# A graph layer and a mixture of experts on one core: late node blocks on two pairs of PSUM banks, 128-row routing scatters, and sort scatters released by TensorE's step signals

## What is computed

```python
def gnn(h, (ei, ej), d2):
    x = concat(h[ei], h[ej], d2)
    msg = silu(x @ mW1 + mb1)
    msg = layer_norm(msg, ln_g, ln_b)
    msg = silu(msg @ mW2 + mb2)
    agg = segment_sum(msg, ei, 6250)
    return h + silu(concat(h, agg) @ uW1 + ub1) @ uW2 + ub2

def moe(tokens):                       # 8 experts, the best 2 of each token
    probs = softmax(tokens @ router_w.T)
    rw, re = top_k(probs, 2);  rw = rw / sum(rw)
    combine = zeros(N, 8) with rw at re
    for e in range(8):
        y = gelu(tokens @ w1[e] + b1[e]) @ w2[e] + b2[e]
        out = out + combine[:, e] * y  # out starts as tokens
    return out

x = x + gnn(_layernorm(x), (src, dst), edge_weight1)
x = x + moe(_layernorm(x))
```

## Time and profile before

| | |
|---|---|
| device time, three runs | 2866.51, 2866.66, 2869.15 us; median 2866.66 |
| profiled execution | 2863.55 us; its span in the profile 2861.8 us |
| busy share of the span | PE 84%, DVE 71%, ACT 53%, POOL 46% |
| mean granted TensorE clock | 0.914 of full speed |
| sort's last matmuls end | 547.2 us |
| late node blocks | 547 to 614 us |
| record conversion | 614.35 to 626.4 us |
| messages, update, router | 626.5 to 2390 us |
| routing scatters | 2392.3 to 2544.4 us |
| first expert matmul, end of span | 2550.2, 2861.8 us |

### The profile page before, as it was taken

One profiled execution on the slowest core, in us unless ns is written; L12 is line 12 of the kernel. 1 busy time (PEld: TensorE's weight loads), 2 busy tenths in 40 slices (PEclk: granted clock), 3 DMA queues, 4 the chain that ended last, 5 costly groups with the idle time before them and its releaser, 6 DMA issues. The chain is left out here.

```text
span 2861.8 us, 60909 instructions
## 1 busy us (share of the span) xinstructions
PE 2391.6 (84%) x15142; PEld 2054.4 (72%) x15143; DVE 2041.0 (71%) x6013; ACT 1506.1 (53%) x5127; POOL 1314.9 (46%) x1333
## 2 busy tenths in 40 slices
PE   4388888768999999999999999999999990039990
PEld 4277777637888888888888888888887880028880
DVE  8989989647777777777777777777777665323335
ACT  2522122237777777777777777777775650013330
POOL 2055555615555555555555555555552114754440
PEclk7599999879999999999999999999999995569995
DMA  6010001123233332223333233323342771333338
GB/s 140 3 30 24 27 24 30 40 81 93 88 90 90 90 90 87 88 89 90 90 89 90 86 88 90 90 88 90 91 84 44 229 239 46 85 93 124 118 104 270
DMA packets 159889, 259.19 MB, mean 91 GB/s; under 512 B 39875, under 2 KB 105088, under 8 KB 159447
## 3 DMA queue, kind: packets, MB, share of 16 engines
q0 software_dynamic: 65392, 139.80, 18.1%
q1 hardware_dynamic: 87392, 111.96, 12.9%
q10 hardware_dynamic: 7025, 6.40, 0.7%
HBM read 195.46 MB, written 62.49 MB: 90 GB/s over the span
## 5 line engine op out<-in xcount | busy, mean ns | idle before, releaser
L966 POOL DMA_INDIRECT work<-dst_half,stage_i x848 | 811.9, 957 | 795.7 <-PE ps L1174 580.1
L1157 PE MATMUL ps<-W2c,work 128*128 128x256 f32 x3392 | 802.3, 379 | 0.0
L1157 PEld LDWEIGHTS ps<-W2c,work 128*128 128x128 f32 x3392 | 612.0, 190 | 70.7
L992 DVE TENSOR_TENSOR agg<-agg,ps 125x256 f32 x848 | 353.3, 417 | 254.7 <-PE ps L1174 244.8
L1098 ACT ACTIVATE work<-ps 128x512 f32<-128x512 f32 x424 | 252.1, 595 | 353.6 <-PE ps L1174 346.6
L1174 PE MATMUL ps<-work 128*125 128x256 f32 x1696 | 435.2, 379 | 1.3 <-ACT work L1119 1.3
L1148 PE MATMUL ps<-ablk,work 128*128 x2544 | 352.2, 275 | 21.7 <-DVE work L1040 11.4
L1113 ACT ACTIVATE work<-work 128x256 f32<-128x256 f32 x848 | 341.4, 404 | 54.5 <-DVE work L1019 50.1
L1071 DVE SCALAR_TENSOR_TENSOR work<-ps,work,b2c 128x256 f32<-128x256 f32 x848 | 368.1, 475 | 0.0
L477 POOL DMA_INDIRECT edge_records<-stage,work x208 | 239.7, 1152 | 265.0 <-ACT stage L768 206.1
L1105 ACT ACTIVATE work<-work 128x256 f32<-128x256 f32 x848 | 340.7, 406 | 2.5 <-issue 2.3
(11 more groups left out here) (274 smaller groups left out, 3262.6 us busy)
## 6 DMA issues: line engine op xcount, KB each, us to landing
work<-tile_sources SPq DMA_DIRECT2D x106, 250.0 KB
work<-routed_tokens SPq DMA_DIRECT2D x53, 257.0 KB
work<-dst_half,stage_i POOLq DMA_INDIRECT x848
routed_tokens<-work SPq DMA_DIRECT2D x26, 514.0 KB
work<-expert_rows SPq DMA_DIRECT2D x25, 320.0 KB, 5.2
update_node_half<-work SPq DMA_DIRECT2D x25, 250.0 KB
work<-update_node_half SPq DMA_DIRECT2D x25, 250.0 KB
work<-expert_rows SPq DMA_DIRECT2D x25, 180.0 KB, 5.9
```

Source lines behind the costliest of these rows:

```text
L966: pool.indirect_dma_start(bg[:, r, u, :], None, dstd, bass.IndirectOffsetOnAxis(ap=stage_i[:, c:c + 1], axis=0)).then_inc(gath[r], 16)
L992: v.tensor_tensor(d, d, ps[0:NB, (7, 0)[a.mod(2)], u * D:(u + 1) * D], ALU.add).then_inc(agg_add, 1)
L1157: last = t_.matmul(ps[:, 5 + s, u * D:(u + 1) * D], sT[:, a.mod(RT), u, k], W2c[:, k], start=(k == 0), stop=(k == KC - 1))
```

## The change

**Late node blocks.** Blocks t of 40 to 49 use banks 6 and 7 when t is even and banks 4 and 5 when it is odd (`ab_bank`, `u_bank`). TensorE turns block t + 1 before it makes the products of block t, and ScalarE copies the turned block t + 1 and scales block t + 2 before it copies out block t. TensorE's waits look one block further back (`last = t - late(t - 1)`; in `turn`, `u_copied` at t - 1). The update halves go out through two buffers in turn by pairs of blocks (`uouts`, `u_buffer`, `u_half`; the second lies in `prods`, which the sort no longer needs by then), with a semaphore for each.

**Blocks 48 and 49** (MID = 48 on) move behind the record conversion on VectorE, ScalarE, TensorE and SyncE. On SyncE that is behind the waits for the scatters and behind the row stores. ScalarE's copies L789 stand before its block 48.

**Sort scatters.** Before scatter k of group g, for all groups but the last, GpSimd waits for TensorE's step m = 5(g + 1) + k // 3 of the next group: for k = 0, 3, 6, 9, 12 for the step's sort matmuls, for k = 1, 4, 7, 10 for the step's node part (`hn_tr` or `ab_ready`). Scatters 2, 5, 8 and 11 follow directly.

**Routing.** The two scatters of a block take all 128 partitions of `ts` and `tslot`. Partitions 125 to 127 go to 24 spare rows behind `routed_tokens`: GpSimd clears partitions 96 to 127 of all of `ts` (2056 floats a partition) and writes the spare row numbers by an iota, and VectorE waits for both before its first block. VectorE's route loop is written out, block by block.

```diff
--- before.py
+++ after.py
@@ -153,7 +153,7 @@
         wcd = nc.dram_tensor("edge_weight_column", (3, D), bf16).ap()
-        xsd = nc.dram_tensor("routed_tokens", (XT * P, XW), f32).ap()
+        xsd = nc.dram_tensor("routed_tokens", (XT * P + 8 * (P - NB), XW), f32).ap()
         yd = nc.dram_tensor("expert_rows", (K2 * N + XD * P, D), f32).ap()
@@ -342,9 +342,35 @@
         u_copied = sem("u_copied")
-        u_stored = sem("u_stored")
+        u_stored = [sem("u_stored0"), sem("u_stored1")]
         LATE = BK - NG * NS // 2
+        MID = BK - 2
+        uouts = [uout, prods[:, 0:KC * 2 * NB].rearrange("p (k u n) -> p k u n", k=KC, u=2)]
+
+        def late(t):
+
+            return t >= BK - LATE
+
+        def ab_bank(t):
+
+            return 4 if late(t) and t % 2 else 6
+
+        def u_bank(t):
+
+            return 5 if late(t) and t % 2 else 7
+
+        def u_half(t):
+
+            return t // 2 % 2 if late(t) else 0
+
+        def u_before(t):
+
+            return sum(u_half(2 * p) == u_half(t - t // BK) for p in range(t // 2))
+
+        def u_buffer(t):
+
+            return uouts[u_half(t)]
@@ -391,14 +417,14 @@
                         sp.dma_start(ud[t // 2].rearrange("p k u n -> p (k u n)"),
-                                     uout.rearrange("p k u n -> p (k u n)")).then_inc(u_stored, 16)
+                                     u_buffer(t).rearrange("p k u n -> p (k u n)")).then_inc(u_stored[u_half(t)], 16)
...
                              mW2.rearrange("(k p) n -> p k n", p=P)).then_inc(w2_in, 16)
-                for t in range(BK - LATE, BK):
+                for t in range(BK - LATE, MID):
                     stores(t)
@@ -412,8 +438,11 @@
+                for t in range(MID, BK):
+                    stores(t)
                 sp.wait_ge(b_stored, 32 * BK)
-                sp.wait_ge(u_stored, 16 * NP2)
+                sp.wait_ge(u_stored[0], 16 * u_before(BK))
+                sp.wait_ge(u_stored[1], 16 * (NP2 - u_before(BK)))
                 sp.wait_ge(wcol_in, 16)
@@ -474,6 +503,11 @@
                     for k in range(KQ):
+                        m = (g + 1) * NS + k // 3
+                        if m < NG * NS and k % 3 == 0:
+                            pool.wait_ge(sorted_ps, m + 1)
+                        elif m < NG * NS and k % 3 == 1:
+                            pool.wait_ge(ab_ready if m % 2 else hn_tr, m // 2 + 1)
                         nc.gpsimd.indirect_dma_start(
@@ -622,7 +656,7 @@
                     wait(dve, c3_ready, t)
-                    v.tensor_tensor(atmp[e], ps[e, 6, 0:D], ablk[e, t, 0], ALU.subtract).then_inc(a_taken, 1)
+                    v.tensor_tensor(atmp[e], ps[e, ab_bank(t), 0:D], ablk[e, t, 0], ALU.subtract).then_inc(a_taken, 1)
@@ -675,10 +709,9 @@
                 link(v.tensor_tensor(b2c[:, :], b2c[:, :], ps[:, 1, 0:D], ALU.add))
-                for t in range(BK - 5, BK):
+                for t in range(BK - 5, MID):
                     third(t - 1)
                     second(t)
-                third(BK - 1)
@@ -700,6 +733,10 @@
                                   ps[:, 2 + h, 0:4 * TP].rearrange("p (k t) -> p k t", k=4)).then_inc(dst_copied, 1)
+                for t in range(MID, BK):
+                    third(t - 1)
+                    second(t)
+                third(BK - 1)
@@ -725,20 +762,20 @@
                     act.wait_ge(hn_tr, t + 1)
-                    nc.scalar.activation(agg[:, t, 0:KC * NB], ps[:, 7, 0:KC * NB], ACT.Copy).then_inc(hnT_ready, 1)
+                    nc.scalar.activation(agg[:, t, 0:KC * NB], ps[:, u_bank(t), 0:KC * NB], ACT.Copy).then_inc(hnT_ready, 1)
...
                     if t % 2 == 0:
-                        wait(act, u_stored, 16 * (t // 2))
-                    nc.scalar.activation(uout[:, :, t % 2, :], ps[:, 7, D:D + KC * NB].rearrange("p (f n) -> p f n", f=KC),
+                        wait(act, u_stored[u_half(t)], 16 * u_before(t))
+                    nc.scalar.activation(u_buffer(t)[:, :, t % 2, :], ps[:, u_bank(t), D:D + KC * NB].rearrange("p (f n) -> p f n", f=KC),
                                          ACT.Copy).then_inc(u_copied, 1)
...
                     act.wait_ge(rank_taken, NS * (min((3 * D * (t + 1) - 1) // (GC * BK), NG - 2) + 1))
-                    nc.scalar.activation(ablk[e, t, 0], ps[e, 6, 0:D], ACT.Copy).then_inc(b_copied, 1)
-                    nc.scalar.activation(agg[e, t, :], ps[e, 6, D:2 * D], ACT.Copy).then_inc(b_copied, 1)
+                    nc.scalar.activation(ablk[e, t, 0], ps[e, ab_bank(t), 0:D], ACT.Copy).then_inc(b_copied, 1)
+                    nc.scalar.activation(agg[e, t, :], ps[e, ab_bank(t), D:2 * D], ACT.Copy).then_inc(b_copied, 1)
@@ -775,19 +812,24 @@
                         halves(t)
+                normal(BK - LATE + 1)
+                turned(BK - LATE)
                 for t in range(BK - LATE, BK):
-                    turned(t)
+                    if t == MID:
+                        act.wait_ge(cols_tr, 1)
+                        for h in range(2):
+                            nc.scalar.activation(rec[:, :, 0].rearrange("p (t k) -> p k t", k=TR)[:, 4 * h:4 * h + 4, :],
+                                                 ps[:, h, 0:4 * TP].rearrange("p (k t) -> p k t", k=4),
+                                                 ACT.Copy).then_inc(rel_copied, 1)
+                    if t + 1 < BK:
+                        turned(t + 1)
                     second(t - 1)
-                    if t + 1 < BK:
-                        normal(t + 1)
+                    if t + 2 < BK:
+                        normal(t + 2)
                     update_half(t)
...
-                act.wait_ge(cols_tr, 1)
-                for h in range(2):
-                    nc.scalar.activation(rec[:, :, 0].rearrange("p (t k) -> p k t", k=TR)[:, 4 * h:4 * h + 4, :],
-                                         ps[:, h, 0:4 * TP].rearrange("p (k t) -> p k t", k=4), ACT.Copy).then_inc(rel_copied, 1)
@@ -828,9 +870,14 @@
                     pe.wait_ge(hn_ready, t + 1)
-                    wait(pe, u_copied, t)
+                    if not late(t - 1):
+                        wait(pe, u_copied, t)
+                    elif late(t - 2):
+                        pe.wait_ge(u_copied, t - 1)
+                    else:
+                        pe.wait_ge(staged, NG)
                     for k in range(KC):
-                        last = t_.transpose(ps[:, 7, k * NB:(k + 1) * NB], agg[e, t, k * P:(k + 1) * P], ident[e, e])
+                        last = t_.transpose(ps[:, u_bank(t), k * NB:(k + 1) * NB], agg[e, t, k * P:(k + 1) * P], ident[e, e])
                     last.then_inc(hn_tr, 1)
@@ -838,14 +885,15 @@
                         for k in range(KC):
-                            last = t_.matmul(ps[:, 7, D + f * NB:D + (f + 1) * NB], uW1h[:, k, f * P:(f + 1) * P], hT[:, k, :],
+                            last = t_.matmul(ps[:, u_bank(t), D + f * NB:D + (f + 1) * NB], uW1h[:, k, f * P:(f + 1) * P], hT[:, k, :],
                                              start=(k == 0), stop=(k == KC - 1))
                     last.then_inc(u_ps, 1)
-                    wait(pe, a_taken, t)
-                    wait(pe, b_copied, 2 * t)
+                    last = t - late(t - 1)
+                    wait(pe, a_taken, last)
+                    wait(pe, b_copied, 2 * last)
                     for k in range(KC):
-                        t_.matmul(ps[e, 6, :], hT[:, k, :], W1ab[:, k, :], start=(k == 0), stop=False)
-                    t_.matmul(ps[e, 6, 0:D], onesh[0:65, e], mbp[0:65], start=False, stop=True).then_inc(ab_ready, 1)
+                        t_.matmul(ps[e, ab_bank(t), :], hT[:, k, :], W1ab[:, k, :], start=(k == 0), stop=False)
+                    t_.matmul(ps[e, ab_bank(t), 0:D], onesh[0:65, e], mbp[0:65], start=False, stop=True).then_inc(ab_ready, 1)
@@ -871,8 +919,9 @@
+                turn(BK - LATE)
                 for t in range(BK - LATE, BK - 5):
-                    turn(t)
+                    turn(t + 1)
                     products(t)
@@ -891,6 +940,10 @@
                     last.then_inc(cols_tr, 1)
+                for t in range(MID, BK):
+                    if t + 1 < BK:
+                        turn(t + 1)
+                    products(t)
                 pe.wait_ge(dst_copied, 2)
@@ -1283,7 +1336,7 @@
                 sp.wait_ge(padrow_set, 2)
-                xsv = xsd.rearrange("(g p) f -> p g f", p=P)
+                xsv = xsd[0:XT * P, :].rearrange("(g p) f -> p g f", p=P)
@@ -1645,6 +1698,7 @@
         ts_ready = sem("ts_ready")
+        ts_spare = sem("ts_spare")
         xt_added = sem("xt_added")
@@ -1673,12 +1727,17 @@
             def _(pool):
+                tail = slice(P // 4 * 3, P)
+                nc.gpsimd.memset(ts[tail], 0.0).then_inc(ts_spare, 1)
+                nc.gpsimd.iota(tslot[tail].rearrange("p r k -> p (r k)"), pattern=[[P - NB, RS * K2]],
```

(10 more changed lines are left out.)

## The result

| | kernel before | changed kernel |
|---|---|---|
| median of the runs | 2867.24 us (4 runs) | 2848.06 us (4 runs, 2843.57 to 2849.36) |
| ratio | | 0.9929, 95% interval 0.9912 to 0.9947 |
| profiled execution, span | 2863.55, 2861.8 us | 2849.16, 2847.4 us |

The change gained 19.2 us in the medians and 14.4 us between the two profiled executions. The forecast was 32.3 us. The time is inside the range, 13.7 us above the forecast, and each of the two parts that were to pay (late blocks and conversion, routing) gave less than its term.

What follows compares the result with a forecast made beforehand. Bounds: VectorE in the sort, GpSimd in routing, the one-bank chain and held signals in the late blocks. 12.5 + 0 + 19.8 = 32.3 us off 2863.55 gives 2831.2; the median, 3.1 above, becomes 2834.4 us (8 in 10: 2821 to 2851).

Steps and rivals of the forecast that it cites:

- the chain: Late blocks, rival: they stay chained, near 4.14 us each; with the conversion they give about 2 us: 2845 us; chance 0.08.
- the row count: Routing, rival against it: row length costs the 0.26 us a scatter, so routing gains nothing: 2856 us; chance 0.09.
- 0.4 us a step: Sort, slower rival: paced scatters hold signals in every step, deciding from 0.4 us in each of 80; 2882 us; chance 0.04.
- the 21 us of the sort's stalls: Sort, rival: VectorE's 3.01 us stalls go with the hold, 21 us more gained: 2813 us; chance 0.07.
- parts 1 and 2: Late blocks in two pairs of banks, and blocks 48 and 49 behind the conversion: 12.5 us saved (8 to 18).
- part 4: Routing: 128 rows instead of 125 in all 100 scatters, less 2.0 us for the start: 19.8 us saved (5 to 24).
- The second weight: Late blocks: from block 44's last matmul to TensorE's last matmul for this weight, 5.0 us, order kept.
- Afterwards the run is 13 long, its first 5 us or so are free, 42 is next at 568.5: End of the sort: blocks 40 and 41 get through on TensorE early in the last scatters; bounds 41 or 43 next.
- C = 595.5: After the late blocks: when the record conversion begins, where it began at 614.35 before.
- cold clock: Late blocks: TensorE restarts at the half clock after idling, 1.5 us added for the whole first block.
- Held until the run ends: Sort and late blocks: a TensorE signal falling late in a long unbroken run of scatters waits for its end.
- part 3: Sort's paced scatters: 0 us in the body; signs were scatters in threes, ScalarE's starts no longer 7 us late, stall kept.

Runs made afterwards that it cites:

- the mixed kernel: The changed kernel without pacing, its scatters of 125 rows in even groups of the sort and even blocks of routing, 128 in the others: 2845.7 us.
- the later addition: The changed kernel without pacing, VectorE's addition in routing one block later: 2814.2 us, ratio 0.9866, where no signals were held.

## Why the prediction was right, and where its sizes were off

- **What bounds each stage**: right. Each part moved its own stage, and none of the rivals came about. Late blocks left the chain, routing gained with the row count, paced scatters took no 0.4 us a step (pacing alone 0.9993), and the 21 us of the sort's stalls did not go.
- **The 17.9 us that the profiled execution gained less than the 32.3 forecast**: 4.9 in parts 1 and 2 (7.6 for 12.5), 8.4 in part 4 (14.0 less 2.6 for the start, for 19.8), 2.6 in messages and router and 2.0 in the rest, which the sum had at nothing. The last two are no more than what one trace differs from the next: over the eight traces with held signals the time from the next stage's first instruction to the router's end is 1758.5 to 1762.0 us, also where the late blocks are unchanged, and what follows the last routing scatter 316.8 to 321.4.
- **The pace of a late block**, 3.2 us: measured 2.94, the bound that I had named, 3.0, and a little under. The second weight took 4.1 us (591.41 - 584.36 - 2.94), not 5.0.
- **"Afterwards the run is 13 long, its first 5 us or so are free, 42 is next at 568.5"** is the step that failed in part 1. That the first microseconds of a run of 13 are free is borne out by the mixed kernel. But the run was 25 long, from 537.52 to 569.99. The pacing doesn't take the group before out of it: its first two scatters wait for TensorE (the second starts at 537.52 after 0.57 us of idle time), TensorE is then ahead of them, and the other eleven and the last 13 follow without a gap. So block 41 is next, as before: one block more, 2.9 us. And the group before started at 535.26, where it started at 530.15 without pacing, so the last 13 start at 553.89, not 549, and block 41's products at 572.89, 4.2 us after the 568.7 that I had for block 42's. I had written that the last group starts no later than its `staged` allows; it started 2.9 us after it, though scatter 12 of the group before, which I had looked at, waited for nothing. Against C = 595.5: +4.2 +2.9, pace -1.6, second weight -0.9, cold clock +1.1 (the first block to the second, 578.47 - 572.89 = 5.6 us, is 2.6 over the pace where 1.5 was taken), together +5.7 of the 5.8 measured. The pacing is not what makes block 41 next: the late blocks alone, unpaced, had it next as well, and gave 8.3 to 17.8 us in the runs.
- **"Held until the run ends"**, which I took from rows 3 and 4: too simple, with no cost in the sum. In the runs of 25 and 26 after the sort ScalarE's starts come 3 to 5 us late while scatters go on (553.62, 556.47 and 561.41 in the changed kernel), and block 40's update half started at 563.60 in the kernel before, ahead of the run's end at 565.62.
- **From the conversion to the next stage**, 18.5 us: 17.65 on the first chip, 16.9 on chip 3.
- **The sort's body**, 0: right. The stall is there with and without held signals, which shows that the hold never fed it. The signs named for part 3 came half: scatters went in runs of up to six rather than in threes, and ScalarE's starts were 1.8 to 2.0 us late instead of 6 to 7.
- **Routing**, 19.8 us: 13.2 in the runs (8.3 to 17.8). The scatter, taken as 1.30 with its gap, is (98.9 + 40.0) / 100 = 1.39 us. The instruction was as sized (0.989), the gap was not: I took that nobody waits for VectorE after the first block, and VectorE now waits for its own held signal, and GpSimd for it. Without held signals the scatter is (96.3 + 31.2) / 100 = 1.275, the stretch 125.5 us, where 125 rows took 148.0 on chip 2, and the term holds. The start cost 2.6, not 2.0.
- **What I treated as a fact of the kernel changed with the chip.** Where signals are held the change gave 19.2 us, on a chip that holds none 41. The forecast, made from a trace of the first kind, lies between, and its range, counted from 2866.66 us, holds both.

No complete kernel here beats the changed one for certain. Without pacing it is the same where signals are held (0.9922 against 0.9929, intervals nearly the same), and with the later addition instead it is the same where they aren't (0.9866 against 0.9855). The later addition was not tried on a chip that holds signals, where it might pay; that stays open.

## What to carry over

Give an indirect scatter a number of rows that 16 divides, with spare rows at a harmless place if need be: 112 and 128 rows cost the same, 125 a quarter to a third more. When a start was ended by "remote", suspect a held signal and ask under which instruction it was. Whether it pays not to let a wait follow its signal directly, where another block's work could stand between, is not tested where signals are held. And when two traces disagree about such a wait, look first at whether the kernel before ran equally fast beside both: a gain measured on one chip need not be that of the next.

## What the runs showed of the hardware

- The sets are of two kinds, and so, it seems, are the chips. The kernel before took 2867.2 and 2870.8 us with held signals (beside the first result and on chip 1; 2863.5 and 2867.8 in the two runs on chip 4), 2851.9 and 2853.3 without (chips 2 and 3). The loop over the messages, too, is some 4 us longer with held signals (from its first matmul to the router's end 1752.5 to 1756.2 us in eight traces, 1748.7 to 1750.8 in the other six).
- With held signals, an engine starts up to 8 us (11 in the run of 25) after the instruction that it waited for. In the sort's body that is mostly 1.2 to 1.8 us after the last scatter of the run; in five odd groups of the kernel before on chip 4 it is 0.2 us before that scatter's end. TensorE's and VectorE's signals are both held, in front of ScalarE, GpSimd and VectorE, and a wait of VectorE for itself is held too.
- Why it comes with the chip, 128 rows and a run, these runs don't tell. All runs record a profile, so that the recording has a share in it is not excluded either.
- Beside a busy VectorE a 128-row scatter takes 1.10 to 1.21 us on average in a group, in the open 0.96. The Trainium skill ("SBUF — State Buffer", Who interferes with whom) names the port pair that VectorE and GpSimd share as the one place of contention, and says that TensorE and ScalarE "never wait on anyone". The traces agree with the first as far as the scatters are longer there. The second is about ports, and held signals are no contention of ports; but whoever reads it as a promise about starts is wrong by those 8 us.
